# The second mixture of experts as a stream of token tiles, gathers of rows waited for by groups, and edges loaded ahead of nodes

## What is computed

```
x = x + L0_gnn(layernorm(x), edges, edge_attr)      # one head, softmax over the edges of a node
x = x + L0_ffn(layernorm(x))                        # shared expert + 2 of 8 experts, hidden 1024
x = x + L1_gnn(layernorm(x), edges)                 # 4 heads, then one head
x = x + L1_ffn(layernorm(x))                        # tokens + 2 of 8 experts, hidden 256
# an expert:  y = gelu(t @ w1[e] + b1[e]) @ w2[e] + b2[e]
# its share:  out = out + combine[:, e] * y         # combine is 0 but for the 2 chosen experts
```

## Time and profile before

| | |
|---|---|
| median of 3 runs | 4366.16 us (4363.21 to 4366.36) |
| the profiled execution | 4368.09 us, its span 4366.3 us |
| mean granted TensorE clock | 0.877 |
| PE, PEld busy | 3580.7 us (82%), 2902.0 us (66%) |
| DVE, ACT, POOL busy | 2637.4 us (60%), 2519.5 us (58%), 813.0 us (19%) |

### The profile page before, as it was taken

The page is one execution under the profiler, slowest core; times in us unless marked ns, Lnnn a source line. Parts: engine busy times, 40 slices in busy tenths (PEclk is TensorE's granted clock), DMA queues, the critical chain, the costliest instruction groups (busy, mean ns, idle before and its releaser), DMA issues. The chain is left out here.

```text
span 4366.3 us, 71110 instructions
## 1 busy us (share of the span) xinstructions
PE 3580.7 (82%) x21458; PEld 2902.0 (66%) x21459; DVE 2637.4 (60%) x5627; ACT 2519.5 (58%) x6453; POOL 813.0 (19%) x464
## 2 busy tenths in 40 slices
PE   4766999989959999962999999999993858886491
PEld 3333555558848999962888888888883747775260
DVE  6877888731141000045999999999986167776212
ACT  3981357840023344334999999999982767773030
POOL 2992000000004000121111111111110011110504
PEclk8556999999969999975999999999997969896595
DMA  4970134564323012113111111111104032311223
GB/s 117 220 192 14 60 150 180 210 243 152 133 72 98 32 57 76 42 59 141 43 49 59 44 44 45 46 49 59 44 13 172 4 138 94 107 65 40 80 83 105
DMA packets 100403, 396.63 MB, mean 91 GB/s; under 512 B 11870, under 2 KB 56386, under 8 KB 77266
## 3 DMA queue, kind: packets, MB, share of 16 engines
q1 hardware_dynamic: 82940, 344.48, 22.9%
q0 software_dynamic: 14976, 44.58, 3.4%
q10 hardware_dynamic: 2368, 6.03, 0.6%
HBM read 270.45 MB, written 124.59 MB: 90 GB/s over the span
## 5 line engine op out<-in xcount | busy, mean ns | idle before, releaser
L1319 PE MATMUL gat_agg<-f_XN,gat_A 128*128 128x257 f32 x5000 | 1110.7, 380 | 21.4 <-DVE gat_A L1436 21.3
L1319 PEld LDWEIGHTS gat_agg<-f_XN,gat_A 128*128 128x128 f32 x5000 | 941.0, 190 | 155.0 <-DVE gat_A L1436 22.1
L1236 ACT ACTIVATE kept_X<-kept_X,gat_s 128x128 f32<-128x128 f32 x2500 | 741.6, 391 | 82.3 <-DVE kept_X L1425 82.3
L2352 ACT ACTIVATE moe_exp_h<-moe_exp_hbank,moe_b1c 128x128 f32<-128x128 f32 x742 | 272.2, 367 | 542.9 <-PE moe_exp_hbank L2303 390.3
L868 PE MATMUL mat_cw<-mat_join,mat_lane 128*128 128x400 f16 x2976 | 511.6, 335 | 34.3 <-issue 18.9
L868 PEld LDWEIGHTS mat_cw<-mat_join,mat_lane 128*128 128x128 f16 x2976 | 290.9, 98 | 255.5 <-issue 48.8
L1425 DVE SCALAR_TENSOR_TENSOR kept_X<-gat_r,gat_s 128x128 f32<-128x128 f32 x1700 | 459.2, 348 | 1.2
L1183 POOL TENSOR_TENSOR kept_X<-gat_low,gat_r 128x1024 f32<-128x1024 f32 x100 | 239.0, 2390 | 1129.4 <-DVE gat_A L1436 683.3
L1808 PE MATMUL gat_agg<-f_XN,gat_A 128*128 128x257 f32 x1250 | 321.3, 420 | 59.4 <-DVE gat_A L1871 59.4
L1389 DVE CUSTOM_DVE_ANT_0 gat_junk<-gat_als,gat_absT 128x3200 bf16<-128x3200 f32 x100 | 348.1, 3481 | 24.9 <-DMA gat_als<-score_rows 18.3
L2310 PE MATMUL moe_exp_ybank<-moe_exp_w2b,moe_exp_h 128*128 128x256 f32 x1484 | 352.3, 387 | 8.3 <-DVE kept_X L2372 5.1
(11 more groups left out here) (365 smaller groups left out, 4868.4 us busy)
## 6 DMA issues: line engine op xcount, KB each, us to landing
gat_C<-count_matrix SPq DMA_DIRECT2D x50, 1600.0 KB, 6.3
count_matrix<-mat_both SPq DMA_DIRECT2D x25, 1600.0 KB, 5.3
weight_matrix<-mat_both SPq DMA_DIRECT2D x25, 1600.0 KB, 8.8
edge_raw<-in_edge_attr_dram SPq DMA_DIRECT2D x50, 768.0 KB, 6.3
e_WT<-weight_matrix SPq DMA_DIRECT2D x13, 1600.0 KB, 6.6
sum_more<-weight_matrix SPq DMA_DIRECT2D x12, 1600.0 KB, 6.7
slot_rows<-moe_exp_xgT POOLq DMA_DIRECT2D x22, 640.0 KB, 3.7
hidden<-gat_h1t SPq DMA_DIRECT2D x25, 512.0 KB, 2.7
```

The source lines that it names most:

```text
L1236: last = nc.scalar.activation(w, w, ACT.Exp, bias=s02[:, t, h:h + 1])
L1319: last = nc.tensor.matmul(agg[h % 2][:, 0:D + 1], A[h % 2][:, t, :], g.XN[:, t, :], start=(t == 0), stop=(t == NT - 1))
L2352: nc.scalar.activation(h[:, f, :], hbank[f % nh][:, 0:P], ACT.Gelu, bias=bias(f)).then_inc(gelu_done, 1)
```

## The change

Four things are changed.

1. In the second mixture the gathers go straight into `xgT`, each with up to four in flight. A new step for each tile, one tile ahead of the item: ACT copies the gathered tile to `cur` (`stage`), PE turns it between the two halves of the item before (`turn_staged`, called as `between`), DVE copies it back over the tile in `xgT` (`copy_staged`). POOL counts `landed` when it has seen a gather's semaphore, which for tile s is just before it issues gather s+4. There is one gather and one turned tile more than slot tiles, for the look ahead. The first mixture keeps its old scheme.
2. In both mixtures the 50 gathers of the rows back wait only once in ten gathers, for the whole group two before.
3. In `prepare` the load of `X` is issued after the stores and reads of the destinations.
4. `xgT` is one tile longer in the second mixture, and `cur` is a new tile.

```diff
...
                 sp.dma_start(to[ER - 1:ER, 0:E_LAST], of[whole:N_EDGES].rearrange("(r w) -> r w", r=1)).then_inc(edges_in, 16)
-            sp.dma_start(X[:, 0:NT - 1, :], a["x"][0:full, :].rearrange("(t p) d -> p t d", p=P)).then_inc(g.x_in, 16)
             sp.wait_ge(dst_ready, 1)
...
             sp.dma_start(nxt, g.dpad[2:2 + E_PAD].rearrange("(r w) -> r w", w=EW)).then_inc(spread, 16)
+            sp.dma_start(X[:, 0:NT - 1, :], a["x"][0:full, :].rearrange("(t p) d -> p t d", p=P)).then_inc(g.x_in, 16)
             sp.wait_ge(packed_ready, 1)
...
 RING = NT
+FLYING = 4
 def experts(nc, sems, tag, g, X, m, w1, w2, shared, KF, n_exp, out):
...
         w2b = [k.sb(f"w2b{b}", [P, KF, D]) for b in range(2 + S)]
-        xgT = k.sb("xgT", [P, SLOT_TILES, D])
+        xgT = k.sb("xgT", [P, SLOT_TILES + (0 if S else 1), D])
+        cur = k.sb("cur", [P, D])
         h = k.sb("h", [P, KF, P])
...
         w_in = [k.sem(f"w_in{b}") for b in range(2 + S)]
-        fetched = [k.sem(f"fetched{b}") for b in range(2)]
+        fetched = [k.sem(f"fetched{b}") for b in range(2 if S else FLYING)]
+        landed, staged = k.sem("landed"), k.sem("staged")
         turned_ready, turned_kept = k.sem("turned_ready"), k.sem("turned_kept")
...
         def _(pool):
-            for s in range(SLOT_TILES):
+            if not S:
+                for s in range(SLOT_TILES + 1):
+                    if s >= FLYING:
+                        pool.wait_ge(fetched[s % FLYING], s // FLYING * 16)
+                        pool.sem_inc(landed, 1)
+                    pool.indirect_dma_start(xgT[:, s, :], None, g.xn_rows[:, :],
+                                            bass.IndirectOffsetOnAxis(m.token[:, s:s + 1], 0)).then_inc(fetched[s % FLYING], 16)
+                for s in range(SLOT_TILES + 1, SLOT_TILES + 1 + FLYING):
+                    pool.wait_ge(fetched[s % FLYING], s // FLYING * 16)
+                    pool.sem_inc(landed, 1)
+            for s in range(SLOT_TILES if S else 0):
                 if s >= 2:
...
                     r = 2 * t + n
-                    if r >= 2:
-                        pool.wait_ge(gathered[(r - 2) // (2 * GROUP)][n], ((r - 2) % (2 * GROUP) // 2 + 1) * 16)
+                    if r % (2 * GROUP) == 0 and r >= 4 * GROUP:
+                        for b in range(2):
+                            pool.wait_ge(gathered[r // (2 * GROUP) - 2][b], GROUP * 16)
                     pool.indirect_dma_start(xgT[:, r, :], None, g.slot_rows[:, :],
...
             pe.sem_inc(y_kept, 1)
-            def multiply(b, item, moving):
+            def turn_staged(t):
+                wait_alone(pe, staged, t + 1)
+                for c in range(KD):
+                    last = nc.tensor.transpose(turned[0][:, c * P:(c + 1) * P], cur[:, c * P:(c + 1) * P], g.ident[:, :])
+                last.then_inc(turned_ready, 1)
+            def multiply(b, item, moving, between=None):
                 for f in range(KF):
...
                     last.then_inc(h_ready, 1)
+                if between is not None:
+                    between()
                 pe.wait_ge(y_kept, item + 1)
...
                 pe.wait_ge(w_in[2], 32)
-            for j, (s0, s1) in enumerate(turns):
-                if S:
-                    multiply(2, j, lambda c: m.xT[:, c, j * P:(j + 1) * P])
+            for j, (s0, s1) in enumerate(turns if S else ()):
+                multiply(2, j, lambda c: m.xT[:, c, j * P:(j + 1) * P])
                 for s in range(s0, s1):
                     turn(s)
-            pe.wait_ge(turned_kept, SLOT_TILES)
+            if S:
+                pe.wait_ge(turned_kept, SLOT_TILES)
+            else:
+                turn_staged(0)
             def item(e, t):
-                multiply(e % 2, t + before, lambda c: xgT[:, at(t), c * P:(c + 1) * P].rearrange("p o n -> p (o n)"))
+                if not S:
+                    wait_alone(pe, turned_kept, t + 1)
+                multiply(e % 2, t + before, lambda c: xgT[:, at(t), c * P:(c + 1) * P].rearrange("p o n -> p (o n)"),
+                         None if S else lambda: turn_staged(t + 1))
             for e in range(E):
...
                 activate(j, of_shared)
-            routed(act, bounds, lambda e, t: activate(t + before, lambda f: m.b1c[:, (e + S) * KF + f:(e + S) * KF + f + 1]))
+            def stage(t):
+                wait_alone(act, landed, t + 1)
+                if not (isinstance(t, int) and t == 0):
+                    wait_alone(act, turned_ready, t)
+                nc.scalar.activation(cur[:, :], xgT[:, at(t), :].rearrange("p o d -> p (o d)"), ACT.Copy).then_inc(staged, 1)
+            def work(e, t):
+                if not S:
+                    stage(t + 1)
+                activate(t + before, lambda f: m.b1c[:, (e + S) * KF + f:(e + S) * KF + f + 1])
+            if not S:
+                stage(0)
+            routed(act, bounds, work)
             if S:
...
                 dve.wait_ge(biased, 1)
-            for j, (s0, s1) in enumerate(turns):
-                if S:
-                    share(j, j)
+            for j, (s0, s1) in enumerate(turns if S else ()):
+                share(j, j)
                 for s in range(s0, s1):
...
                     nc.vector.tensor_copy(xgT[:, s, :], turned[s % 2][:, 0:D]).then_inc(turned_kept, 1)
+            def copy_staged(t):
+                wait_alone(dve, turned_ready, t + 1)
+                nc.vector.tensor_copy(xgT[:, at(t), :].rearrange("p o d -> p (o d)"), turned[0][:, 0:D]).then_inc(turned_kept, 1)
             def keep(e, t):
+                if not S:
+                    copy_staged(t + 1)
                 wait_alone(dve, h_used, (t + before) * KF + 2 * KF)
...
                                         ALU.add).then_inc(y_kept, 1)
+            if not S:
+                copy_staged(0)
             routed(dve, bounds, keep)
...
```

## The result

The changed kernel took 4252.19 us (median of 4, 4249.05 to 4255.23) beside 4364.68 us for the kernel before (4 runs, 4362.24 to 4366.36) on the same chip: a ratio of 0.9743, 95% interval 0.9726 to 0.976. That is 112.5 us less, 3 us from the forecast of 4249. On another chip, on which a later experiment fell, the same kernel took 4378.59 us, 18 us more than the kernel before beside it (4360.18), and four near copies of it were slower than the kernel before on yet another one. Both are results of this change; the first is read first.

What follows compares the result with a forecast made beforehand. No engine was full: the kernel's end was 58 gathers, some 55 items and 50 gathers in series. Terms -84.7 - 16.3 - 12.9 - 3.4 = -117.3 us gave 4249 us against the median, range 4234 to 4276 at 0.87.

Steps and rivals of the forecast that it cites:

- Step 1: Second mixture: token gathers stream beside the items instead of preceding them; -84.7 us, bounds -91.5 and -33.
- what an item pays: Second mixture's items: turning and copying the next tile adds 0.10 us an item over 53 items, +5.3 us.
- term of 1.5 us for a slow clock at the start: First two items of the second mixture: they run at the slow clock and cost 1.5 us more.
- so I take 0.07 for them: Loop end of each item on PE: one more instruction and two more register waits cost 0.07 us.
- the cover of DVE's copy: Each item: the turned tile's copy is done at S+2.0 and wanted at S+2.3, 0.3 us to spare.
- rival B: Items: turn, DVE's copy and next item form a chain, 2.7 to 2.9 us an item, about 4268 us; chance 0.13.
- Step 2: Rows back in both mixtures: gathers 1.265 us apart; -16.3 us in the second mixture, -12.9 in the first.
- the two are level: End of first mixture's rows back: tenth shared tile done at 1892, last gather landed at 1892.8; 0.6 us given away.
- Step 3: In `prepare`: edges load ahead of `X`, so DVE's edge work starts earlier; -3.4 us, bounds 0 and -11.
- Both covers: In `prepare`: `X` lands 12 us before it is wanted, the packed edges 1 us before.
- one case slower than before: Items: Copy and Gelu alternating on ACT need two table loads each, +141 us, 4390 us; chance 0.02.
- It fits: Rows back: transfers at 105 GB/s plus the stores of `out` take about half of the DMA time.

Runs made afterwards that it cites:

- back_three: The changed kernel with each gather of the rows back waited for three behind; 4380.84 us, ratio 1.0048 to the kernel before.
- edges_wide: The changed kernel with each load of 111 rows of edges split into 96 and 15 rows; 4242.37 us, ratio 0.9731 to the kernel before.
- edges_only: The kernel before with only the load of `X` moved behind the reads of the padded destinations; 4356.54 us, ratio 0.9993.
- changed_again: The changed kernel unaltered, run on another chip; 4378.59 us, ratio 1.0045 to the kernel before.
- two_ahead_wait: The changed kernel with token tiles turned two ahead, PE's wait at each item's head kept; 4381.09 us, ratio 1.0037 to the kernel before.
- two_ahead: The changed kernel with token tiles turned two ahead and PE's wait at each item's head removed; 4372.55 us, ratio 1.0014 to the kernel before.
- wait_twice: The changed kernel with PE's wait for the turned tile and its nop written twice per item; 4383.71 us, ratio 1.0043 to the kernel before.
- stream_only: The changed kernel with the rows back and the load of `X` as before, leaving the second mixture's stream alone; 4282.81 us, ratio 0.9818.
- back_only: The kernel before with only the rows back waited for by whole groups; 4334.42 us, ratio 0.994.

## Why the prediction was right, and where it was not

By its steps, on the first chip:

- **Step 1**, first item: started 5.89 us after the first gather (4032.43 - 4026.54) in place of 98.30, a gain of 92.4 where 91.5 was forecast. Right.
- **Step 1**, what an item pays: +0.19 us, not +0.10; from the first item's start to the last addition 136.7 us in place of 126.6, +10.1 where +6.8 was forecast. The transposes and both copies were covered, as argued. The term of 1.5 us for a slow clock at the start did not come: the first item took 0.40 us more to its addition and the second 0.60 less, the clock being up sooner. Mis-sized was the sentence "so I take 0.07 for them": the wait on a register with its nop cost 0.19, 10 us over 53 items. And the cover of DVE's copy was not 0.3 us but 0.06: the prediction compared the copy's end with the next item's start and left out the hand-over of 0.35, which rival B had used. B was not the bound, by 0.06 us.
- **Step 2**: 1.270 and 1.266 us between gathers for 1.265 forecast. Second mixture -16.3, as forecast; first mixture -12.8 (-12.9), its last additions released by the last shared tile (1890.87) and no longer by a gather, as the prediction had it ("the two are level"). That only two or three gathers need be in flight holds in the first mixture (back_three: 1.260 us, with DVE mostly idle beside it) and less in the second, where three gave 1.342.
- **Step 3**: -4.3 us at the first edge operation, -3.4 forecast; 2.1 of them left at 1826 us in this pair of traces (by the means of all traces, 3.3 of 4.5). edges_wide bears out that the loads used few engines, and edges_only that `X` slowed them. That it did so by its traffic on the other engines is the prediction's argument; no run shows it. Both covers held: ACT's first load of edge features came 4.30 us earlier (42.37 us), as did the store of packed edges ahead of it (30.96).
- **Sum**: -116.2 in the span, -117.3 forecast. 2.7 us of it came between 1905 and 4026 us, in stretches that the change does not touch. They are chance: from the first gather back to the second mixture's first token gather, edges_only, with the same code there as before, took 2210.78 us and before 2215.98. That the sum is off by 1.1 us is luck in this part: these 2.7 stood against the 3.3 that the items cost beyond the forecast.

What it had no notion of is the stall. Its rivals held one case slower than before, for another reason, at 2 in 100. The step that failed there is "It fits", behind the DMA share: it asked whether transfers and engines have room beside an unbroken stream of gathers, and never whether signals between the engines do. On the chip of changed_again the stream is worth 14.4 us (224.86 to 210.43) and not 82.3, and the stretch with the first mixture's rows back is 44.2 us longer than before (2215.98 to 2260.13) in place of 15.5 shorter. Why PE's signals are late there stays open.

## What to carry to other kernels

When a phase is pulled under another, its work mostly hides and its waits do not: count each wait on the busiest engine's queue (0.19 us here, 10 us over 53 items) and look for one that another wait already implies. Count the hand-over into a cover. And when an engine is to issue DMAs without a pause beside engines that signal one another closely, time the kernel on more than one chip: the same program was 2.6% faster or 0.45% slower than the one it replaces. And before a microsecond is put down to a change, see how much the same event moves between traces that lack it (here 1826.92 to 1829.06 us at one gather).

## What the hardware showed that was not expected

- On two of the chips met (the changed kernel itself on one, near copies on both), TensorE's semaphore increments arrived 10 to 20 us late while POOL issued an indirect gather every 1.25 us; signals from ACT to PE took 0.05 us in the same stretch. On the others nothing of it. Whether it is the chip or what it held at the time was not told apart.
- An indirect gather of 128 rows of 1 KB costs POOL 0.95 us and 0.30 of "issue", with 3, 4 or more in flight alike; while DVE adds beside it, 1.01 to 1.12.
- A PE wait with its nop costs 0.20 us though its semaphore is long met (two_ahead_wait, 2.43 us, against two_ahead, 2.23), and written a second time 0.10 more (wait_twice).
- At the same point of the program, after the same work, the TensorE clock rose from half to full at moments more than a microsecond apart from one execution to the next: from PE's first weight load of the stretch to its fourth product there were 5.86 us in before, 6.92 in stream_only and 6.44 in back_only, in all three with the edges loaded alike; the granted clock rose 3.9 us after that load in before and 5.0 in back_only.
